# Attention scores in three PSUM banks, every second head's penalty written by ScalarE, and the rows of maxima sent by SyncE

## The reference, cut to what matters

```python
def _L0_xattn_ref(queries, keys, values, mask, W_q, W_k, W_v, W_proj, b_proj):
    Q = (queries @ W_q.T).reshape(b, sq, N_HEADS, D_HEAD).transpose(0, 2, 1, 3)
    ...
    scores = jnp.einsum('bhqd,bhkd->bhqk', Q, K) / scale
    scores = jnp.where(mask, scores, NEG_INF)
    attention = jax.nn.softmax(scores, axis=-1)
    heads_out = jnp.einsum('bhqk,bhkd->bhqd', attention, V)
    ...
x = x + jnp.tanh(g_xattn[0]) * _L0_xattn_ref(_layernorm(x), ctx, ctx, mask, ...)
x = x + jnp.tanh(g_ffn[0]) * _L0_ffn_ref(_layernorm(x), ...)          # 256 -> 768 -> 256, quantized
x = x + jnp.tanh(g_xattn[1]) * _L1_xattn_ref(_layernorm(x), ctx, ctx, ...)   # no mask
x = x + jnp.tanh(g_ffn[1]) * _L1_ffn_ref(_layernorm(x), ...)          # 32 experts, capacity 160
```

## Time and profile before

| | |
|---|---|
| median of 3 runs | 1262.97 us (1260.5 to 1263.43) |
| the profiled execution's own time | 1267.7 us |
| its span, first to last instruction | 1266.4 us, mean granted TensorE clock 0.983 |
| layer 0, 11 items in the middle (106.2 to 388.3 us) | 25.65 us each |
| layer 1, 12 items in the middle (787.6 to 1064.2 us) | 23.05 us each |
| TensorE matmuls busy | 1188.2 us, 94% |
| VectorE, ScalarE, GpSimd busy | 70%, 56%, 38% |

### The profile page before, as it was taken

How to read it: one execution, slowest core, us unless ns; L and a number is a source line. 1 busy time by engine, 2 the same in 40 slices (tenths; PEclk the granted TensorE clock), 3 DMA queues, 4 the chain that set the end, 5 groups by cost and what they waited for, 6 DMA issues and landing times.

```text
span 1266.4 us, 25147 instructions
## 1 busy us (share of the span) xinstructions
PE 1188.2 (94%) x9260; PEld 877.5 (69%) x9260; DVE 892.3 (70%) x2680; ACT 709.8 (56%) x1197; POOL 480.1 (38%) x677
## 2 busy tenths in 40 slices
PE   7799999999999989999999978999999999889998
PEld 6577777777777654444458866777777777578987
DVE  4687878877788446599999846768778778642343
ACT  2356556565656538899964425666666666622221
POOL 5445434443342000166001433443643643323555
PEclk9899999999999989999999999999999999988999
DMA  7424333433331050000004643364563442147973
GB/s 188 136 62 126 106 107 89 114 111 88 115 87 54 19 176 1 1 1 1 1 25 143 184 134 105 106 169 131 154 172 112 134 129 61 52 160 250 304 193 37
DMA packets 121941, 137.23 MB, mean 108 GB/s; under 512 B 12881, under 2 KB 116427, under 8 KB 121797
## 3 DMA queue, kind: packets, MB, share of 16 engines
q1 hardware_dynamic: 111888, 125.98, 33.5%
q0 software_dynamic: 7296, 8.15, 3.5%
q10 hardware_dynamic: 2634, 1.49, 0.5%
HBM read 58.42 MB, written 27.36 MB: 68 GB/s over the span
## 4 chain that ended last, share of the span: by engine, by line
PE 72%; DVE 9%; ACT 6%; issue 6%; POOL 3%; DMA 1%; ACTq 1%; SPq 1%; another core or an unknown queue 0%; POOLq 0%; DVEq 0%
PE PS L676 14%; PE PS L477 8%; PE PS L418 7%; PE PS L461 6%; PE PS L722 6%; PE PS L437 6%; PE PS L690 4%; PE PS L509 4%; PE PS L535 4%; PE PS L464 3%; PE PS L425 3%; ACT P L846 2%; PE PS L731 2%; DVE MX L1123 2%; DVE ON L1181 2%
## 5 line engine op out<-in xcount | busy, mean ns | idle before, releaser
L846 ACT ACTIVATE P<-PS 128x512 f32<-128x512 f32 x512 | 300.0, 602 | 125.0 <-PE PS L464 75.7
L461 PE MATMUL PS<-QS,KS 99*128 99x256 bf16 x1024 | 226.7, 274 | 14.4 <-ACT P L846 13.3
L1123 DVE CUSTOM_DVE_ANT_0 MX<-PS,NQ 128x256 bf16<-128x256 f32 x512 | 191.8, 417 | 56.1 <-PE PS L437 56.1
L1126 DVE TENSOR_REDUCE NM<-PS 128x2 f32<-128x512 f32 x256 | 172.2, 684 | 64.9 <-PE PS L437 64.5
L437 PE MATMUL PS<-KS,QS 96*128 96x256 bf16 x1024 | 195.4, 274 | 5.9 <-DMA QS<-PP 2.1
L461 PEld LDWEIGHTS PS<-QS,KS 99*128 99x128 bf16 x1024 | 92.7, 99 | 61.6 <-issue 23.3
L464 PE MATMUL PS<-NK,identb 128*128 128x256 bf16 x512 | 127.9, 274 | 0.0
L477 PE MATMUL PS<-P,V 128*32 128x256 f32 x2048 | 125.5, 386 | 1.2 <-ACT P L846 1.2
L676 PE MATMUL PS<-XNT,wup 128*128 128x512 f16 x576 | 124.9, 379 | 0.0
L437 PEld LDWEIGHTS PS<-KS,QS 96*128 96x128 bf16 x1024 | 96.6, 98 | 36.8 <-issue 10.2
L676 PEld LDWEIGHTS PS<-XNT,wup 128*128 128x128 f16 x576 | 56.2, 98 | 67.4
(11 more groups left out here) (234 smaller groups left out, 2465.1 us busy)
## 6 DMA issues: line engine op xcount, KB each, us to landing
KS<-PP SPq DMA_DIRECT2D x192, 128.0 KB, 3.1
QS<-PP SPq DMA_DIRECT2D x192, 128.0 KB, 2.7
WH<-in_wex SPq DMA_DIRECT2D x16, 768.0 KB
WG<-in_wex SPq DMA_DIRECT2D x10, 768.0 KB
bufd<-bias_row SPq DMA_DIRECT2D x5, 1032.0 KB, 12.4
XB<-in_x SPq DMA_DIRECT2D x16, 256.0 KB, 3.4
CT<-in_ctxT SPq DMA_DIRECT2D x16, 256.0 KB, 3.1
x1d<-XB SPq DMA_DIRECT2D x16, 256.0 KB, 2.1
```

Of the source, the lines that this page charges most:

```text
L461: ins = tensor.matmul(o, t.KS[b % 3][0:99, h, 128 * kt:128 * kt + 128], t.QS[b % 3][0:99, h, :], start=True, stop=(L == 1))
L846: scalar.activation(t.P[i % NP_RING][:, :, :], PS[:, h % 2, :].rearrange("p (k n) -> p k n", k=2), ACT.Exp).then_inc(s_ex, 1)
L1123: ins = vector.tensor_tensor_reduce(t.MX[:, 2 * score_turn(L, b, h) + qt, :], PS[:, bk, 256 * qt:256 * qt + 256], t.NQ[b % 4][:, qt, :], - ...
L1126: ins = vector.tensor_reduce(nm[:, :, h], PS[:, bk, :].rearrange("p (t n) -> p t n", t=2), X, ALU.max, negate=True)
```

## The change

- Both kinds of scores turn over three banks: 2, 3, 4 for the ones with queries on the partitions, 0, 1, 5 for the transposed ones. A transposed head now waits for the exponential of the head three before it. The product with V loses its own bank and takes one of the alternating pair 6 and 7.
- In layer 0, for every odd head (but head 1 of item 0), ScalarE writes the penalty NK into the head's PSUM bank with a copy, 3 heads ahead, and the two matmuls of the scores add onto it. That is 127 heads; the two matmuls with the identity fall away there. Even heads get one identity matmul of 512 columns, ahead of the scores, in place of two of 256.
- The product with V and the copy of its result (`pe_av`, `act_heads`) stand first in slots 9 and 1, ahead of the head's scores and exponential.
- The DMA of the maxima's rows is issued by SyncE, in slots 10 and 2, after the loads of that slot and ahead of the stacks.
- Semaphores are merged to make room for the new one (d_m with d_xe into d_in, d_x1 with d_xf into d_out, s_pad dropped); warm-up matmuls write another bank.

```diff
 def score_bank(L, b, h):
...
-    return (2, 3, 5)[score_turn(L, b, h)]
+    return 2 + turn_of(L, b, h)
...
+def laid_first(b, h):
+    return h % 2 == 1 and (b, h) != (0, 1)
+def score_t_bank(L, b, h):
+    return (0, 1, 5)[turn_of(L, b, h)]
...
         def pe_scores_t(L, b, h):
...
-            pe.wait_ge(s_ex, i - 1)
+            pe.wait_ge(s_ex, i - 2)
             if L == 0:
                 pe.wait_ge(s_pen, n + 1)
-            bk = h % 2
+            if L == 0 and laid_first(b, h):
+                pe.wait_ge(s_pre, i // 2)
+            bk = score_t_bank(L, b, h)
+            laid = L == 0 and laid_first(b, h)
+            if L == 0 and not laid:
+                tensor.matmul(PS[:, bk, :], identb[:, :], t.NK[b % 4][:, :, :].rearrange("p k n -> p (k n)"),
+                              start=True, stop=True)
             for kt in range(2):
-                o = PS[:, bk, 256 * kt:256 * kt + 256]
-                ins = tensor.matmul(o, t.KS[b % 3][0:99, h, 128 * kt:128 * kt + 128], t.QS[b % 3][0:99, h, :],
-                                    start=True, stop=(L == 1))
-                if L == 0:
-                    ins = tensor.matmul(o, identb[:, :], t.NK[b % 4][:, kt, :], start=False, stop=True)
+                ins = tensor.matmul(PS[:, bk, 256 * kt:256 * kt + 256], t.KS[b % 3][0:99, h, 128 * kt:128 * kt + 128],
+                                    t.QS[b % 3][0:99, h, :], start=(L == 1), stop=True, skip_group_check=(L == 0))
...
         def pe_av(L, b, hh):
+            bk = odd_bank(("av", n, hh), s_ot, 2 * n + hh + 1)
...
         def pe_slot(L, s, k):
+            if 0 <= s < NB and k == 9:
+                pe_av(L, s, 0)
+            if 0 <= s - 1 < NB and k == 1:
+                pe_av(L, s - 1, 1)
             if 0 <= s < NB:
                 pe_scores_t(L, s, k)
-                if k == 9:
-                    pe_av(L, s, 0)
...
+        def act_penalty(b, h):
+            i = 16 * b + h
+            act.wait_ge(s_pen, b + 1)
+            act.wait_ge(s_ex, i - 2)
+            scalar.activation(PS[:, score_t_bank(0, b, h), :].rearrange("p (k n) -> p k n", k=2), t0.NK[b % 4][:, :, :],
+                              ACT.Copy).then_inc(s_pre, 1)
...
         def act_maxima(L, b, hh):
...
-            act.wait_ge(s_nt, 2 * n + hh + 1)
-            act.wait_ge(s_st, 16 * (n - 2))
-            scalar.dma_start(t.QS[b % 3][96:99, 8 * hh:8 * hh + 8, :], t.NT[hh][:, :]).then_inc(d_n[hh][b % 3], 16)
...
         def act_slot(L, s, k):
+            if 0 <= s < NB and k == 9:
+                act_heads(L, s, 0)
+            if 0 <= s - 1 < NB and k == 1:
+                act_heads(L, s - 1, 1)
             if 0 <= s < NB:
                 act_exp(L, s, k)
+            ahead = 16 * s + k + 3
+            if L == 0 and 0 <= ahead < 16 * NB and laid_first(*divmod(ahead, 16)):
+                act_penalty(ahead // 16, ahead % 16)
...
+        def sp_maxima(L, b, hh):
+            n, t = L * NB + b, TL[L]
+            sp.wait_ge(s_nt, 2 * n + hh + 1)
+            sp.wait_ge(s_st, 16 * (n - 2))
+            sync.dma_start(t.QS[b % 3][96:99, 8 * hh:8 * hh + 8, :], t.NT[hh][:, :]).then_inc(d_n[hh][b % 3], 16)
```

More of the change, by code:

```diff
@@ L102, in scores_at, with turn_of @@
     return (k,)
-def score_turn(L, b, h):
+def turn_of(L, b, h):
     return (16 * (L * NB + b) + h) % 3
@@ L343, in build @@
         d_c = [sem(f"d_c{i}") for i in range(2)]
-        d_m = [sem(f"d_m{i}") for i in range(2)]
+        d_in = [sem(f"d_in{i}") for i in range(2)]
         d_w = {n: sem("d_w" + n) for n in "qkvo"}
@@ L355, in build @@
         s_evar, s_ers, s_xm, s_xmp, s_xmt = (sem(n) for n in ("s_evar", "s_ers", "s_xm", "s_xmp", "s_xmt"))
-        d_x1 = [sem(f"d_x1{i}") for i in range(4)]
+        d_out = [sem(f"d_out{i}") for i in range(4)]
         s_am = sem("s_am")
@@ L371, in build @@
         d_sc = [sem(f"d_sc{i}") for i in range(2)]
-        d_xe = [sem(f"d_xe{i}") for i in range(2)]
-        d_xf = [sem(f"d_xf{i}") for i in range(4)]
         s_et, s_xet, s_eg, s_si, s_eu, s_he, s_ey, s_ix, s_ye = (sem(n) for n in (
@@ L393, in rows_in @@
             if q == 0:
-                return (d_xf[0], 32) if i in (0, 4) else (d_xf[i], 16)
-            return d_xe[q % 2], 80 * (q // 2 + q % 2)
+                return (d_out[0], 96) if i in (0, 4) else (d_out[i], 80)
+            return d_in[q % 2], 16 * (NB // 2) + 80 * (q // 2 + q % 2)
         def odd_bank(job, emptier, value):
@@ L476, in pe_av @@
                         h = 8 * hh + 4 * g + i
-                        ins = tensor.matmul(PS[32 * i:32 * i + 32, 4, 256 * g:256 * g + 256], t.V[b % 3][:, kt, h, :],
+                        ins = tensor.matmul(PS[32 * i:32 * i + 32, bk, 256 * g:256 * g + 256], t.V[b % 3][:, kt, h, :],
                                             t.P[(16 * n + h) % NP_RING][:, kt, :], start=(kt == 0), stop=(kt == 1))
@@ L601, in pe_slot @@
                     if L == 1 and s == NB:
-                        pe_warm(4, 6)
+                        pe_warm(5, 6)
                     pe_out(L, s - 1)
@@ L606, in pe_slot @@
                     if s - 2 == NB - 1:
-                        pe_warm(4, 14)
+                        pe_warm(5, 14)
                     pe_xm(L, s - 2)
@@ L612, in pe_slot @@
                     if s - 2 == NB - 1:
-                        pe_warm(4, 10)
+                        pe_warm(5, 10)
                     pe_ranks(GROUP_OF[s - 2][0])
@@ L759, in pe_program @@
             pe.wait_ge(s_cst, 1)
-            pe_warm(4, 20)
+            pe_warm(5, 20)
             for s, k in slots(0):
                 pe_slot(0, s, k)
-            pe_warm(4, 6)
+            pe_warm(5, 6)
             pe.wait_ge(s_am, NB)
@@ L766, in pe_program @@
             pe_scale_b(0)
-            pe_warm(4, 13)
+            pe_warm(5, 13)
             for i in range(NCH):
@@ L803, in pe_program @@
             pe.wait_ge(s_pos, 6)
-            pe_warm(4, 30)
+            pe_warm(5, 30)
             pe_turn(0)
@@ L935, in act_slot @@
         def act_slot(L, s, k):
+            if 0 <= s < NB and k == 9:
+                act_heads(L, s, 0)
+            if 0 <= s - 1 < NB and k == 1:
+                act_heads(L, s - 1, 1)
             if 0 <= s < NB:
                 act_exp(L, s, k)
+            ahead = 16 * s + k + 3
+            if L == 0 and 0 <= ahead < 16 * NB and laid_first(*divmod(ahead, 16)):
+                act_penalty(ahead // 16, ahead % 16)
             for b, hh in maxima_at(L, s, k, 10, 2):
                 act_maxima(L, b, hh)
-            if 0 <= s < NB and k == 10:
-                act_heads(L, s, 0)
             for b, kk in heads_at(L, s, k):
@@ L1136, in dve_any @@
             t = t0
-            dve.wait_ge(d_m[b % 2], 16 * uses(0, b, 2))
+            dve.wait_ge(d_in[b % 2], 16 * uses(0, b, 2))
             dve.wait_ge(s_rs, b - 1)
@@ L1448, in dve_ffn @@
             for i in range(4):
-                dve.wait_ge(d_x1[i], 64)
+                dve.wait_ge(d_out[i], 64)
             dve.wait_ge(s_am, NB)
@@ L1621, in pool_masks @@
             t = t0
-            pool.wait_ge(d_m[b % 2], 16 * uses(0, b, 2))
+            pool.wait_ge(d_in[b % 2], 16 * uses(0, b, 2))
             pool.wait_ge(s_mx, 16 * (b - 3))
@@ L1819, in sp_stack @@
                                    PP[1 - which][:, part, :, :].rearrange("p m n -> p (m n)")).then_inc(stacked[b % 3], 16)
+        def sp_maxima(L, b, hh):
[3 more added lines that the diff above has]
+            sync.dma_start(t.QS[b % 3][96:99, 8 * hh:8 * hh + 8, :], t.NT[hh][:, :]).then_inc(d_n[hh][b % 3], 16)
         def sp_x1(b):
             sp.wait_ge(s_res, b + 1)
-            sync.dma_start(rows(x1d, b), t0.XB[b % 5][:, :, :]).then_inc(d_x1[b % 4], 16)
+            sync.dma_start(rows(x1d, b), t0.XB[b % 5][:, :, :]).then_inc(d_out[b % 4], 16)
         def sp_base(b):
@@ L1885, in sp_slot @@
                     sp_load_mask(s + 3)
+            for b, hh in maxima_at(L, s, k, 10, 2):
+                sp_maxima(L, b, hh)
             if (L, s, k) == (0, -2, 14):
@@ L1906, in sp_x1_load @@
         def sp_x1_load(b):
-            sp.wait_ge(d_x1[b % 4], 16 * uses(0, b, 4))
+            sp.wait_ge(d_out[b % 4], 16 * uses(0, b, 4))
             if b >= 3:
@@ L1939, in sp_program @@
                 sp_expert_rows(e)
-            sp.wait_ge(d_xf[0], 32)
+            sp.wait_ge(d_out[0], 96)
             for e in range(4, 8):
```

26 lines of the change are left out of this document (10 added, 16 removed).

## The result

The changed kernel takes 1240.77 us, the median of 4 runs (1238.87 to 1243.41), against 1262.92 us before. The ratio is 0.983, with a 95% interval of 0.9808 to 0.9852: faster by 22 us or 1.7%, where 32.5 us had been forecast. In both, TensorE stood at the lower of its two clock levels (1.2 in place of 2.4 GHz) for 43.7 us in all, though not in the same places.

A forecast was written before the change was run, and what follows sets the result against it. TensorE was taken as the bound, 96% busy mid-attention, except for ON's wait on VectorE. Terms of -19.1 us in layer 0 and -13.4 in layer 1 gave -32.5: predicted 1231 us, range 1214 to 1252.

The forecast's parts named there:

- The identity matmuls, 28.2 us off TensorE: In layer 0, 127 heads lose two identity matmuls of 0.111 us each: 28.2 us, 1.78 us an item.
- Heads 5 and 7 given back to ON: Between queries and ON, VectorE sets the pace, so these heads' saving returns as ON's wait: 5.8 us.
- The sign given for it, a longer wait at ON: In layer 0's slot 8, ON's wait on VectorE should remain, a little longer, by up to 0.44 us.
- ScalarE's penalties cost nothing in the middle: In layer 0, eight copies an item, 0.60 us each, are covered by the slots with fp32 work.
- The new tie of the product with V to banks 6 and 7 costs nothing by the list.: In slot 10 the output projection's wait for a copy, 0.7 us after the product, hides behind 1.2 us of matmuls.
- Layer 0's last item, 1.5 us: Penalties may come onto the path at layer 0's end, 0 to 5.0 us; 1.5 us was counted as cost.
- Layer 1, 11.1 and 2.3 us: Late starts of 0.19 and 0.55 us go in 15 items, 11.1 us; moving the DMA saves 2.3 at the end.
- The 2.3 us for the DMA at the end: In layer 1's last two items ScalarE leads; freeing it of the DMA gains 3 x 0.78 = 2.3 us (0 to 4).
- The DMA moved to SyncE costs nothing: On SyncE the stacks start up to 4 us later, but the next item needs them some 12 us after.
- rival D: The maxima's rows land late behind SyncE's loads in layer 1; 8 items lose 1 us each: 1239 us; chance 0.06.
- Rival B: VectorE becomes the bound; in layer 0 only heads beside fp32 work gain: -16.5 us, about 1246; chance 0.12.
- Rival C: ScalarE's PSUM write is dear, making ScalarE the bound from about 1.05 us; at 1.2 us, 1282; chance 0.06.

The follow-up runs named there:

- e2_no57: Changed kernel without ScalarE's penalty for heads 5 and 7 (95 heads in place of 127): 1240.3 us, ratio 0.9777 to the kernel before.
- e1_nopen: Changed kernel without any ScalarE penalty; every head of layer 0 gets its identity columns from TensorE: 1250.5 us, ratio 0.9871 to the kernel before.
- e9_nolast: Changed kernel without ScalarE's penalty in layer 0's last item only: 1239.6 us, ratio 0.9799 to the kernel before.
- e3_actdma: Changed kernel with the DMA of the maxima's rows issued by ScalarE again: 1245.1 us, ratio 0.9846 to the kernel before.
- e7_b_sp: Kernel before with only the DMA of the maxima's rows moved to SyncE: 1261.7 us, ratio 0.9967 to the kernel before.
- e8_pen2: Changed kernel with every penalty written twice, the second copy waiting for the first: 1266.4 us, ratio 1.0009 to the kernel before.

## Why the prediction was right, and where it was off

The direction, the main mechanisms and the range were right; the size was 10 us too large by the medians and 5.5 by the two traces. That the two traces come nearer is in part luck: the profiled execution of the kernel before is 4.8 us above its median, that of the changed kernel is at its median.

- *The identity matmuls, 28.2 us off TensorE.* Right in kind. In the seven items between 5 and 12 without transposes the mean gain is 1.3 us. 1.78 less what ON takes back, 0.36 on average, is 1.42.
- *Heads 5 and 7 given back to ON.* Right in size: e2_no57 is level with the changed kernel. The sign given for it, a longer wait at ON, is not in the plain items (0.33 us in item 5 after, 0.36 before); part of it stands at the transposes of OT.
- *ScalarE's penalties cost nothing in the middle.* The price of 0.60 us and the pace were right, and ScalarE was not the bound in the changed kernel's plain items. The cover was thinner than said: with the DMA back as well, plain items lose 0.4 us, and with the penalty doubled they wait for ScalarE.
- *"The new tie of the product with V to banks 6 and 7 costs nothing by the list."* This is the step that failed. I looked at one neighbour, the output projection, and took an item's jobs as always the same. In items 3, 4, 9 and at the end the weights' transposes put an odd number of jobs between, and the alternation hands the product a bank just filled. In the 11 items the product waits 2.8 + 1.7 us for it, and the weights' transposes 1.3 us. This is not all loss, since other waits shrink: e1_nopen against the kernel before puts the price at about 2 us.
  The sum counted 1.42 us an item, 15.6 for the 11 items, and 8.9 came. Of the 6.7 us missing, 3.0 are in items 3, 4 and 9, the clock taken off, and 1.7 are the lower clock in item 3. Item 2, which has no transposes, misses 1.0: its ON waits 2.2 us for VectorE, as before. The seven plain items miss 0.15 us each, 1.0 in all. The rest of layer 0 brought 0.2 us more than counted. So the tie is the largest part that I left out, but not the whole.
- *Layer 0's last item, 1.5 us.* Agrees, within what e9_nolast can tell.
- *Layer 1, 11.1 and 2.3 us.* The mechanism is right, 0.73 us in nine plain items, but the total came out by luck. It was counted for 15 items. Nine bring 6.7 us, items 5 and 9 nothing, items 0 and 1 together 2.9 and the last two distances 2.6. Behind the last product with V come another 2.7 us, where the kernel before spends 6.8 us more at the lower clock, worth up to 3.4. The 2.3 us for the DMA at the end show in neither e3_actdma nor e7_b_sp.
- *The DMA moved to SyncE costs nothing.* Right in the middle of the stages, wrong at layer 1's start: one wait of 3.6 us, rival D in another place than it was expected. The stage between layer 0 and the first product with V grew by only 0.5 us, since the kernel before waits for other DMAs there, 4.0 us.

Rival B, VectorE as the bound, holds for the stretch from the queries to ON; waits for its maxima come to 1.6 us of the 11 items besides. Rival C needed a penalty of more than 1.05 us; e8_pen2 has about 1.23 and is level with the kernel before, where C's own sum gives about 22 us more. So the turning point lies higher than C had it, and the way there was another one: waits at the pair of banks in a few items.

## What to carry to other kernels

When a job loses its own buffer and joins a rotation, follow the rotation through every variant of the loop, not only the common one: an odd number of rare jobs between two regular ones shifts who waits for whom, and each wait names the engine that empties the buffer, not the data that the job reads. When work moves to another engine's list, look at what stands ahead of it there: here rows that were ready waited 5.1 us for their turn to be sent. Work added to an engine that is 20 to 40% idle is free only as long as no other engine waits for what stands behind it in its list. And before a saving is counted in full, cut the loop at the places where another engine sets the pace, since what is saved ahead of such a place comes back as its wait.
